# Recurrence, steps 1 to 6: the order of the y projection and of the bounded projection of the next step's rows on TensorE

## The reference, cut to what matters

```python
# block 2, "bounded": on rows x of block 1
out = (x @ weight) * scale
v_norm = max(norm(out), EPS)
out = out * tanh(v_norm) / (v_norm + EPS)
out = out * min(0.99 / max(norm(out), EPS), 1.0)
x = layernorm(x + out)
# block 3, recurrence: on those rows, 4 sequences of 512
y      = gelu(x @ w_y + b_y)
conv   = conv_b + sum_k conv_w[k] * shifted(x @ w_x + b_x, k)      # 4 taps
gate_x = sigmoid(conv @ w_ig + b_ig)
gate_a = sigmoid(conv @ w_ag + b_ag)
a      = exp(-8 * gate_a * softplus(a_param))
nx     = gate_x * conv * sqrt(1 - a * a)
h[t]   = a[t] * h[t-1] + nx[t]
x      = layernorm(x + (h * y) @ w_out + b_out)
```

## Time and profile before

| | |
|---|---|
| median of 3 runs | 1020.6 us (1020.0 to 1021.3) |
| the profiled execution, its own time | 1019.97 us |
| its span, first to last instruction | 1018.2 us |
| mean granted TensorE clock | 0.991 |
| blocks 2 and 3 in steps 1 to 6 | about 448 to 657 us of the span |

### The profile page before, as it was taken

One profiled execution on the slowest core, in us unless ns is written; L12 is line 12 of the kernel. 1 busy time (PEld: TensorE's weight loads), 2 busy tenths in 40 slices (PEclk: granted clock), 3 DMA queues, 4 the chain that ended last, 5 costly groups with the idle time before them and its releaser, 6 DMA issues.

```text
span 1018.2 us, 19736 instructions
## 1 busy us (share of the span) xinstructions
PE 990.5 (97%) x7412; PEld 803.3 (79%) x7412; DVE 806.1 (79%) x1431; ACT 658.9 (65%) x1352; POOL 331.7 (33%) x462
## 2 busy tenths in 40 slices
PE   5899999999999999899999999999999999999997
PEld 5889898989999897689788878975546875875873
DVE  6998999999999999867766866785868766766763
ACT  7968787868687778565675566766233762761750
POOL 2004243241524244443435343423421330331331
PEclk9799999999999999999999999999999999999999
DMA  7531404050440336321011102133602002101001
GB/s 228 201 111 32 146 2 164 10 169 6 172 152 13 134 115 233 138 84 42 1 45 42 34 10 70 46 104 104 219 20 84 31 1 87 39 2 63 21 1 62
DMA packets 45279, 82.42 MB, mean 81 GB/s; under 512 B 7424, under 2 KB 17664, under 8 KB 43136
## 3 DMA queue, kind: packets, MB, share of 16 engines
q1 hardware_dynamic: 45184, 81.16, 23.5%
HBM read 68.29 MB, written 12.85 MB: 80 GB/s over the span
## 4 chain that ended last, share of the span: by engine, by line
PE 85%; DVE 6%; ACT 4%; issue 2%; POOL 2%; DMA 0%; SPq 0%; POOLq 0%; DVEq 0%; ACTq 0%
PE banks L869 25%; PE banks L1643 16%; PE banks L2314 14%; PE banks L2384 8%; PE banks L1611 6%; PE banks L2305 5%; PE banks L1016 2%; PE banks L1008 1%; PE banks L964 1%; PE banks L993 1%; DVE c_cv L1459 1%; PE banks L1629 1%; PE banks L2285 1%; PE banks L1604 1%; PE banks L891 0%
## 5 line engine op out<-in xcount | busy, mean ns | idle before, releaser
L2384 PE MATMUL banks<-d_wd,d_hh 128*128 128x512 f16 x256 | 97.1, 379 | 0.0
L2384 PE MATMUL banks<-d_wd,d_hl 128*128 128x512 f16 x256 | 97.0, 379 | 0.0
L696 DVE SCALAR_TENSOR_TENSOR a_xs<-a_xpre,a_cvec,a_xs 128x256 f32<-128x256 f32 x192 | 92.5, 546 | 0.5 <-ACT a_xs L486 0.4
L1958 POOL TENSOR_TENSOR d_hl<-d_h32s,d_hh 128x512 f16<-128x512 f32 x48 | 55.6, 1158 | 97.4 <-ACT d_hh L2053 97.4
L869 PE MATMUL banks<-a_xth,a_wgh 128*128 128x256 f32 x256 | 75.6, 295 | 1.8 <-DVE a_wgl L632 1.8
L721 DVE TENSOR_TENSOR_SCAN a_L<-a_L,a_ident 128x512 f32<-128x512 f32 x64 | 74.8, 1211 | 0.5
L869 PE MATMUL banks<-a_xth,a_wxh 128*128 128x256 f32 x256 | 74.4, 290 | 0.0
L869 PE MATMUL banks<-a_xth,a_wgl 128*128 128x256 f32 x256 | 73.6, 287 | 0.0
L869 PE MATMUL banks<-a_xtl,a_wgh 128*128 128x256 f32 x256 | 73.5, 287 | 0.0
L869 PE MATMUL banks<-a_xtl,a_wxh 128*128 128x256 f32 x256 | 72.3, 282 | 0.0
L869 PE MATMUL banks<-a_xth,a_wxl 128*128 128x256 f32 x256 | 72.2, 282 | 0.0
(11 more groups left out here) (374 smaller groups left out, 3261.1 us busy)
## 6 DMA issues: line engine op xcount, KB each, us to landing
a_L<-decays SPq DMA_DIRECT2D x16, 1024.0 KB, 4.7
a_xf<-in_x_turned SPq DMA_DIRECT2D x16, 256.0 KB, 3.7
a_xr<-in_x SPq DMA_DIRECT2D x16, 256.0 KB, 2.7
tokens<-a_xr SPq DMA_DIRECT2D x16, 256.0 KB, 2.2
c_xb<-tokens SPq DMA_DIRECT2D x16, 256.0 KB, 2.7
d_xin<-tokens SPq DMA_DIRECT2D x16, 256.0 KB, 4.4
d_r<-tokens SPq DMA_DIRECT2D x16, 256.0 KB, 2.8
d_wd_codes<-in_down_w SPq DMA_DIRECT2D x4, 1024.0 KB, 9.3
```

What stands on the lines that cost most here:

```text
L696: ins = dve.scalar_tensor_tensor(out=out, in0=xpre[:, m, k:k + T], scalar=cvec[:, m, k:k + 1], in1=out, op0=ALU.mult, op1=ALU.add)
L1958: pool.tensor_tensor(hl[:, m, :], (h32s[:, m % 4, :] if i else h32[:, m % 2, :]), hh[:, m, :], ALU.subtract).then_inc(s_hl, 1)
L2384: ins = pe.matmul(ps_o[:, c % 2, :], h[:, m, cols(c)], wd[:, m, :], start=(m == 0 and h is hh), stop=(m == M - 1 and h is hl), skip_group_ ...
```

## The change

In steps 1 to 6 TensorE runs `project` y first and `bounded(s + 1)` second. Step 0 keeps its order, and step 7 has no `bounded`. No instruction is added or removed, and the other engines' streams are as they were.

```diff
                 project(ps_a, W["x"], xth, xtl, lambda q: wait(pe, s_ga, M * (s - 1) + 2 * q + 2), s_xb,
                         None if s else (s_xl, C), None if s else lambda: after_sums(turn_in))
-                if s + 1 < NS:
+                if s == 0:
                     bounded(s + 1)
-                if s == 0:
                     pe.wait_ge(*split["y"])
                     pe.wait_ge(*last["residual"])
                 project(ps_b, W["y"], xth, xtl, lambda q: wait(pe, s_gx, M * (s - 1) + 2 * q + 2), s_yp)
+                if 0 < s < NS - 1:
+                    bounded(s + 1)
                 if s + 1 == NS:
                     following_stage["gate_up"](0, 0)
                 if s:
                     output(s - 1)
```

## The result

The changed kernel takes 1039.45 us (median of 4 runs, 1035.82 to 1040.39), the kernel before it 1020.3 us (4 runs, 1019.66 to 1021.3). The ratio is 1.018, with a 95% interval of 1.0168 to 1.0192: slower by 1.8%. The forecast was 1037.6 us with a range of 1035.0 to 1041.0. The profiled execution took 1039.72 us.

The account below looks back on a forecast made before the run. TensorE was taken as the bound. To 1020.6 us the forecast added 13.25 us for steps 1 to 5, 2.15 for step 6 and 1.6 for clock falls, 17.0 together: 1037.6 us, range 1035.0 to 1041.0.

Parts of the forecast that it names:

- TensorE is the bound and has nothing to gain: Step 2: TensorE is busy 34.66 of 34.70 us, so reordering its own work can only lose.
- VectorE waits for the second chunk, 2.65 us later: VectorE's second scaling of bounded's product cannot start before 498.83, so low_hy and the convolution behind it end 2.65 us later.
- Output 2.15 late with a gap of 1.9, then ag 2.65 late by cvh: TensorE idles 1.9 us before output, waiting for hyl; then ag waits for cvh, leaving TensorE 2.65 us late.
- Paid in each step: No later step gets the wait back: 5 x 2.65 = 13.25 us for steps 1 to 5.
- The loop term: Added waiting without clock loss: 13.25 us in steps 1 to 5 and 2.15 in step 6, 15.4 us together.
- Step 6: 2.15 us: In step 6, 16 transposes between output and ag cover the convolution, so only the wait for hyl costs: 2.15 us.
- Step 7 has no bounded projection and shifts as a whole: Step 7 was expected to start later with everything moved alike, adding no further cost.
- The clock: Falls of TensorE's granted clock behind one or two of six new 1.9 us gaps: 1.6 us.
- The clock never falls: Rival: the new gaps cost no clock in any step, 1036.0 us; chance 0.24.
- Only the wait for hyl counts: Rival: the convolution catches up, so six steps lose 2.15 us each, 12.9 us, giving 1033.5 us; chance 0.06.
- It falls in every step: Rival: the granted clock falls behind all six new gaps, costing 6.95 us, giving 1042.9 us; chance 0.05.
- Not slower: Rival: VectorE reaches the scaling later than the trace shows, so bounded is in time, 1020.6 us; chance 0.03.

Follow-up runs that it names:

- half way: Against the kernel before, bounded stands behind 24 of the 48 matmuls of y in steps 1 to 6: 1020.91 us, ratio 1.0006.
- second-chunk: Against the kernel before, only the second chunk of bounded (12 matmuls) moves behind y in steps 1 to 6: 1039.33 us, ratio 1.0179.
- three-quarters: Against the kernel before, bounded stands behind 36 of the 48 matmuls of y in steps 1 to 6: 1028.18 us, ratio 1.0077.
- three changed steps: Against the kernel before, y and bounded are exchanged in steps 1 to 3 alone; steps 4 to 6 keep the old order: 1028.45 us, ratio 1.0083.
- gap-filled: Changed kernel plus 8 matmuls with unread results behind bounded in steps 1 to 6: 1036.12 us, ratio 1.0152 to the kernel before.
- tanh earlier: Changed kernel with four convolution instructions ahead of VectorE's scalings, low_hy between them, and tanh between the gelu halves on ScalarE: 1025.56 us, ratio 1.0053.
- the two other kernels: Changed kernel with VectorE's low_hy ahead of both scalings, 1030.88 us; changed kernel with convolution begun before the scalings, low_hy between them, 1030.13 us.

## Why the prediction was right, point by point

*TensorE is the bound and has nothing to gain.* Right: no kernel with another order was faster, and half way the time was the same within 0.15%.

*VectorE waits for the second chunk, 2.65 us later.* Right in place and size. The idle times of 0.58 and 1.90 us, released by TensorE, are those forecast (0.5 and 2). The second-chunk and three-quarters kernels show that this wait alone decides, from the point that the rows of before had given.

*Output 2.15 late with a gap of 1.9, then ag 2.65 late by cvh.* Right: the gaps are 1.91 and 1.92 us. Steps without a fall of the clock last 37.41 us, 2.66 above 34.75. The forecast idle of 0.4 us ahead of ag is 0.22 and 0.28 us in steps 4 and 5. It is absent in steps 1 to 3, where the slower clock keeps output running beyond cvh (in step 2 output ends at 511.62, cvh at 510.26).

*Paid in each step.* Right, by the kernel with three changed steps. The loop term of 15.4 us measured 15.6 in the gap-filled kernel's median.

*Step 6: 2.15 us.* The shift between the start of step 6 and ag of step 7 is 2.5 us, 0.4 more. The step of the prediction that failed is "Step 7 has no bounded projection and shifts as a whole". VectorE and GpSimd do not shift alike there. The two rows of before, first, and the two of after:

```profile
658.28 0.69 DVE L2109 TENSOR_SCALAR d_wu_first<-d_wu_early_codes 128x1024 f16<-128x1024 int32 x1
...
658.34 2.84 POOL L1283 TENSOR_TENSOR c_gx<-c_gx,c_cv 128x1024 f32<-128x1024 f32 x1 [4.99 <-ACT c_gx L1340]
```

```profile
676.67 2.85 DVE L2110 TENSOR_SCALAR d_wu_first<-d_wu_early_codes 128x1024 f16<-128x1024 int32 x1
...
676.17 2.80 POOL L1283 TENSOR_TENSOR c_gx<-c_gx,c_cv 128x1024 f32<-128x1024 f32 x1 [4.42 <-ACT c_gx L1340]
```

Before, a conversion of block 4's weights slipped in 0.06 us ahead of GpSimd's product and took 0.69 us. After, it starts 0.50 us behind that product's start and takes 2.85 us, until 679.5, and the recurrence of step 6 stands behind it. Counted from the start of step 6, VectorE had come 2.69 us later and GpSimd, released by ScalarE, 2.13. The other traces fall in line. Where the conversion starts ahead of the product (three steps) or 0.01 us behind it (half way), it takes 0.69 us. Where it starts 0.4 to 0.6 us behind (changed, second chunk, gap filled, three quarters, tanh earlier), it takes 2.84 or 2.85 us and ends 0.54 to 0.56 us behind the product, and ag of step 7 is late by 0.4 us more than output of step 6 was, against 0.0 with three steps. In the two other kernels VectorE is earlier, and it is the conversion ahead of this one that starts 0.5 and 0.7 us behind the product, takes 2.63 us and ends 0.55 us behind it. No kernel was made to separate this overlap from the rest.

*The clock.* Right in kind, mis-sized in both factors. The number of falls in the profiled execution was three, not one or two, and a fourth, in step 7, was not in the sum. The price of one in steps 1 to 5 is 38.15 - 37.41 = 0.74 us, not 1.05. Output loses 1.84 us (7.39 against 5.55), of which 1.1 is covered and not 0.7: the two groups of ag ahead of cvl take 0.69 us and not 0.96 when they run without a pause. The forecast's own 1.7 less 0.7 gives 1.0, not 1.05. 3 x 0.74 = 2.2 us and 1.6 us behind ag of step 7 make 3.8 us in this execution, 3.3 in the medians, against a forecast of 1.6. The sum left out that a gap the kernel had already, of 1.5 us, could be followed by a fall too: one execution of before had shown it without. Whether the change has a part in that fall is open, since the half-way kernel's profile has it as well.

The measured loss is 1039.45 - 1020.3 = 19.15 us against the 17.0 of the sum. Of the 2.15 us between them, 1.7 are clock and 0.4 the step 7 term. The median came out only 1.85 us above the forecast, since the kernel before ran 0.3 us faster beside it (1020.3) than in the runs that the forecast started from (1020.6).

The Trainium skill, "TensorE: Matmul & The Clock Gate", section "HAM oscillation — how this bites in real kernels", taken strictly, allowed no fall behind gaps this short. The runs do not agree with that reading: three of six gaps of 1.9 us and one of 1.55 us were followed by a fall, and with the gaps filled there was none.

*The rivals.* "The clock never falls" (1036.0) is what one of four runs did (1035.82). "Only the wait for hyl counts" (1033.5) is out: each step without a fall lasts 2.66 us longer, not 2.15. The convolution does not catch up. "It falls in every step" (1042.9) is out: behind three of the six gaps the clock stayed at 1.00. "Not slower" is out.

## What to carry to other kernels

When one engine is full, a new order of its own work cannot gain and can lose: list for each thing it hands out who reads it, what that reader would do at that moment, and what is queued behind the read; the slack (here 2.6 us) could be read from one trace to within 0.1 us, and beyond it every microsecond is paid, in each turn of the loop. Moving half as far may cost nothing, and moving half of the work may cost everything, so ask which instruction of a block the reader waits for. Where such a wait opens an idle gap on TensorE, add a term for the granted clock and price it as a spread, since equal gaps are followed by a fall in some steps and not in others.

## What the runs showed of the hardware that was not expected

- A gap of 1.91 us on TensorE was followed by half clock in three steps, and an equal one in three others was not. With the second chunk alone it was steps 1, 2 and 5 and not 1, 2 and 3, and with three changed steps none of three. In step 7 the clock fell behind a gap of 1.55 us here and of 1.57 us half way, and not behind one of 1.56 us in the three-quarters kernel. Nor does the length of a gap order them: in step 0 of the half-way kernel a gap of 2.69 us was followed by no fall, where the earlier trace rows had a fall behind 2.43 us. The forecast's ranking of gaps by length rested on too few of them.

```profile
434.81 0.74 PE L1643 MATMUL banks<-c_cvh,c_wagh 128*128 128x256 f32 x4 [2.69 <-ACT c_cvh L1335]
```

```profile
434.00:439.00 5.00, 4.15 (x32) 1.00 1.02 410
```

- A kernel with 48 more matmuls was faster (1036.12 against 1039.45 us), with the granted clock at 1.00 behind all six gaps that they filled.
- A GpSimd instruction that starts inside VectorE's low_conv, a subtraction of two tensors in SBUF of 1024 values a partition, ends only behind that one's end: it took 1.77 us in place of 0.71 for L1241, 1.20 in place of 0.24 for L1242. One that had started ahead of low_conv was not held (L1241 at 505.13, 0.71 us). The Trainium skill, "GPSIMD Engine Reference", section "1. Specifications", says that GpSimd's access to SBUF is shared with VectorE and names VectorE instructions with two SBUF inputs as a case of contention; by that rule these rows agree.
- The other way round, VectorE's conversion of 1024 integers a partition took 2.85 us in place of 0.69 us beside a GpSimd product of two tensors, whenever it started 0.4 us or more behind it (five traces, and two more with the conversion ahead of it), and ended 0.54 to 0.56 us behind the product.
